# Second attention: even heads' probabilities transposed by VectorE blocks and DMAs, odd heads' by TensorE

## The reference, cut to what matters

```python
    q = (x @ Wq).reshape(b, t, h, dh).transpose(0, 2, 1, 3)
    k = (x @ Wk).reshape(b, t, h, dh).transpose(0, 2, 1, 3)
    wv = _topk_mask(gl_v, SEL) * jax.nn.sigmoid(gl_v)          # gl_v = x @ Ws
    xv = jnp.einsum('btd,edk->btek', x, Wv)
    v = jnp.einsum('bthe,btek->bhtk', wv, xv)
    scores = jnp.einsum('bhid,bhjd->bhij', q * scale, k)
    probs = jax.nn.softmax(scores, axis=-1)
    attn = jnp.einsum('bhij,bhjd->bihd', probs, v)
    mask_o = _topk_mask(gl_o, SEL)                             # gl_o = x @ Wd
    out = jnp.einsum('bthe,bthk,ekd->btd', mask_o, attn, Wo)
```

## Time and profile before

| | |
|---|---|
| Time, median of 3 runs | 1181.05 us (1181.04 to 1181.17) |
| The profiled execution, first to last instruction (its span) | 1179.4 us |
| What lies around the span, by that median | 1.7 us |
| PE busy | 1166.3 us, 99% |
| DVE, ACT, POOL busy | 71%, 55%, 56% |

### The profile page before, as it was taken

The page is one execution under the profiler, slowest core; times in us unless marked ns, Lnnn a source line. Parts: engine busy times, 40 slices in busy tenths (PEclk is TensorE's granted clock), DMA queues, the critical chain, the costliest instruction groups (busy, mean ns, idle before and its releaser), DMA issues.

```text
span 1179.4 us, 19711 instructions
## 1 busy us (share of the span) xinstructions
PE 1166.3 (99%) x6381; PEld 909.4 (77%) x6381; DVE 834.1 (71%) x1524; ACT 650.8 (55%) x1456; POOL 659.0 (56%) x476
## 2 busy tenths in 40 slices
PE   7999999999999999999999999999999999999998
PEld 6888888888888888877767777677677777777765
DVE  7988787878787857465675765666666765765768
ACT  7634343434343434477656666556657666665654
POOL 2635242424242425459298297397397396495595
PEclk9999999999999999999999999999999999999999
DMA  5441423232323224401002002002002011010021
GB/s 198 144 132 46 134 63 115 67 111 73 105 79 99 80 63 155 153 6 37 1 1 107 0 18 89 0 25 81 0 36 71 0 56 51 0 71 0 0 71 37
DMA packets 40893, 75.92 MB, mean 64 GB/s; under 512 B 3744, under 2 KB 4512, under 8 KB 40864
## 3 DMA queue, kind: packets, MB, share of 16 engines
q1 hardware_dynamic: 40864, 75.55, 19.1%
HBM read 58.76 MB, written 16.78 MB: 64 GB/s over the span
## 4 chain that ended last, share of the span: by engine, by line
PE 93%; DVE 4%; ACT 1%; issue 1%; DMA 0%; DVEq 0%
PE ps_f L992 22%; PE ps_r L2081 13%; PE ps_o L2151 9%; PE ps_s L2138 8%; PE ps_s L2130 8%; PE ps_s L992 7%; PE ps_h L992 6%; PE ps_r L2090 6%; PE ps_r L2114 4%; PE ps_r L2096 1%; PE ps_r L2072 1%; PE ps_r L2104 1%; DVE z_tmp L1764 1%; DVE z L1764 1%; PE ps_t L1051 1%
## 5 line engine op out<-in xcount | busy, mean ns | idle before, releaser
L1750 DVE TENSOR_REDUCE nmax<-ps_s 128x1 f32<-128x512 f32 x256 | 158.7, 682 | 112.9 <-PE ps_s L2130 111.9
L1581 ACT ACTIVATE tmp<-ps_s,nmax 128x512 f32<-128x512 f32 x256 | 172.7, 687 | 94.0 <-DVE nmax L1750 94.0
L1524 POOL TENSOR_TENSOR z<-z,z_tmp 128x1280 f32<-128x1280 f32 x35 | 102.9, 2939 | 166.3 <-DVE z_tmp L1764 164.0
L1506 POOL TENSOR_TENSOR spare<-xv,pick 128x512 f32<-128x512 f32 x160 | 169.4, 1059 | 35.6 <-DVE pick L1859 22.7
L1512 POOL TENSOR_TENSOR spare<-spare 128x512 f32<-128x512 f32 x128 | 181.6, 1419 | 10.0
L1590 ACT ACTIVATE pt<-ps_s 128x512 f32<-128x512 f32 x256 | 132.1, 612 | 10.5 <-PE ps_s L2138 10.5
L2138 PE MATMUL ps_s<-ident,tmp 128*128 128x128 f32 x1024 | 122.3, 273 | 0.0
L2138 PEld LDWEIGHTS ps_s<-ident,tmp 128*128 128x128 f32 x1024 | 115.4, 140 | 8.6 <-issue 1.6
L2151 PE MATMUL ps_o<-pt,spare 128*64 128x512 f32 x496 | 113.3, 598 | 0.0
L254 POOL TENSOR_TENSOR e_t<-e_t 128x512 fp32r<-128x512 f32 x28 | 35.4, 1301 | 135.6 <-ACT e_t L510 135.6
L2130 PE MATMUL ps_s<-k,q 64*128 64x512 f32 x768 | 107.0, 409 | 0.1
(11 more groups left out here) (235 smaller groups left out, 2125.4 us busy)
## 6 DMA issues: line engine op xcount, KB each, us to landing
stage<-in_x SPq DMA_DIRECT2D x32, 256.0 KB, 3.3
x_sb<-in_x SPq DMA_DIRECT2D x8, 1024.0 KB, 5.4
x_dram<-x_sb SPq DMA_DIRECT2D x32, 256.0 KB, 3.1
stage<-x_dram SPq DMA_DIRECT2D x8, 1024.0 KB, 5.6
x_sb<-x_dram SPq DMA_DIRECT2D x8, 1024.0 KB, 5.7
out_dram<-x_sb SPq DMA_DIRECT2D x31, 256.0 KB, 2.0
stage<-in_ctx_t SPq DMA_DIRECT2D x28, 256.0 KB, 2.9
stage<-in_ctx SPq DMA_DIRECT2D x28, 256.0 KB, 2.7
```

What stands on the lines that cost most here:

```text
L1506: pool.tensor_tensor(v_tmp[:] if e else acc, xv[:, :, e, :].unsqueeze(2).broadcast_to(shape), pick[:, 0, e, :, 2 * p:2 * p + 2].unsqueeze( ...
L1524: pool.tensor_tensor(zv, zv, z_tmp[:, h % 2], ALU.add).then_inc(z_pool, 1)
L1581: act.activation(probs[:, n % BANKS, :], ps_s[:, n % BANKS, :], ACT.Exp, bias=nmax[:, n:n + 1], accum_out=den[:, h, t:t + 1]).then_inc(p_e ...
L1750: dve.tensor_reduce(nmax[:, n:n + 1], ps_s[:, n % BANKS, :], AX_X, ALU.max, negate=True).then_inc(nmax_ready, 1)
```

## The change

The two tiles of even heads in each round are no longer transposed by PE and copied by ACT. DVE transposes each in place in SBUF, in blocks of 32x32, and then DMAs of SP's queue carry the blocks to the partitions on which they belong in `pt`: 16 DMAs for each round, one for each pair of source and destination quarter of the partitions. Each has 32 partitions with 4 pieces of 64 elements, 256 bytes, so 32 KB. The columns of a head in `pt` are ordered quarter, query tile, element within the block instead of query tile, element; ACT's copy of the odd tiles writes this order, and the copy of the product with v (`out_copy`) puts it back.

The probabilities of even heads have two rounds of buffer (the old `tmp`), those of odd heads one round (a new `probs_odd`). The exponential of an even tile waits for the DMAs of the round two before (`moved`), and `values` waits for the moved blocks of both rounds of its pair. `scores` waits for the copy of the odd tile alone. The last two rounds of the last item go as before, on PE and ACT.

To make room in SBUF, the unused part of `z_t2` is dropped, `halves` becomes the smaller `better` (the count over the experts' comparisons takes 4 additions of 320 elements instead of 3, one of them of 640), and the output mask has its own bf16 buffer `mask` instead of half of `pick`.

```diff
+        def even_probs(n):
+            return probs_even[:, n // BANKS % 2, :, n % BANKS // 2, :]
...
+        def turned(n):
+            h, t = head_tile(n)
+            return pt[:, h % 4].rearrange("p k (q t a) -> p k q t a", q=QUADS, a=BLOCK)[:, :, :, t, :]
...
+        MOVED = QUADS * QUADS * 16
...
+            def move_blocks(b, r, first=False):
+
+                p, tiles = r // 2, slice(r % 2 * 2 * BLOCK, r % 2 * 2 * BLOCK + 2 * BLOCK)
+                sp.wait_ge(blocks_turned, b * ODD_STEPS + (r + 1) * ODD_ROUND)
+                if first and p == 2:
+
+                    sp.wait_ge(o_ps, p - 1)
+                for q in range(QUADS):
+                    for j in range(QUADS):
+                        out = pt[j * BLOCK:(j + 1) * BLOCK, 2 * p % 4].rearrange("p k (q u) -> p k q u", q=QUADS)
+                        sp.dma_start(out[:, :, q, tiles],
+                                     probs_even[q * BLOCK:(q + 1) * BLOCK, r % 2].rearrange(
+                                         "p (k j) s a -> p k j (s a)", j=QUADS)[:, :, j, :]).then_inc(moved[r % 2], 16)
+
             def steady(b, more):
-                if more:
-
-                    sp.wait_ge(yt_ps, b * NT + 2 * NT)
-                    load_x1(b + 2)
+                for r in range(CUT, ROUNDS):
+                    move_blocks(b, r)
+                    if more and r == CUT + 1:
+
+                        sp.wait_ge(yt_ps, b * NT + 2 * NT)
+                        load_x1(b + 2)
+                for r in range(CUT):
+                    move_blocks(b + 1, r)
                 store(b)
...
             def scores_exp(b, n, first):
                 act.wait_ge(nmax_ready, b * STEPS + n + 1)
...
+                if n % 2 == 0:
+                    if n >= 2 * BANKS or not first:
+
+                        act.wait_ge(moved[n // BANKS % 2], (b * PAIRS + n // PAIR) * MOVED)
+                    out, scores = even_probs(n), scores.rearrange("p (j a) -> p j a", a=BLOCK)
...
-                        for tile in range(n * BANKS, n * BANKS + BANKS):
+                        for tile in range(n * BANKS + 1, n * BANKS + BANKS, 2):
                             probs_copy(b, tile, first)
...
+            def turn_blocks(b, n):
+
+                dve.wait_ge(p_exp, b * STEPS + n + 1)
+                dve.transpose(even_probs(n), even_probs(n)).then_inc(blocks_turned, 1)
+
...
                 elif place == TURNS:
+                    if 0 <= n < ROUNDS:
+                        for tile in range(n * BANKS, n * BANKS + BANKS, 2):
+                            turn_blocks(b, tile)
                     if n == LAST_SUMS_AT[0]:
                         mix_sum(b, H - 2)
...
-                pe.wait_ge(pt_ready, b * STEPS + PAIR * p + PAIR)
+                pe.wait_ge(pt_ready, odd_turned(b, PAIR * p + PAIR - 1))
+                for r in range(2):
+                    pe.wait_ge(moved[r], (b * PAIRS + p + 1) * MOVED)
                 pe.wait_ge(v_steps, (b * PAIRS + p + 1) * V_STEPS)
...
                     elif place == TURNS:
-                        for tile in range(n * BANKS, n * BANKS + BANKS):
+                        for tile in range(n * BANKS + 1, n * BANKS + BANKS, 2):
                             turn_probs(b, tile)
```

More of the change, by code:

```diff
@@ L1206, in expert_attention @@
     PLACES = range(5)
+    BLOCK, QUADS = 32, P // 32
     def head_tile(n):
@@ L1348, in expert_attention @@
         pt_ready = sem("pt_ready")
+        blocks_turned = sem("blocks_turned")
+        moved = [sem(f"moved{r}") for r in range(2)]
         o_ps = sem("o_ps")
@@ L1471, in _ @@
             load_x1(1)
+            for r in range(CUT):
+                move_blocks(0, r, True)
             with sp.Fori(0, B - 2) as b:
@@ L1576, in scores_exp @@
                 act.wait_ge(nmax_ready, b * STEPS + n + 1)
-                if n >= BANKS or not first:
-                    act.wait_ge(pt_ps, b * STEPS + n - BANKS + 1)
                 h, t = head_tile(n)
-                act.activation(probs[:, n % BANKS, :], ps_s[:, n % BANKS, :], ACT.Exp, bias=nmax[:, n:n + 1],
+                scores = ps_s[:, n % BANKS, :]
+                if n % 2 == 0:
+                    if n >= 2 * BANKS or not first:
+                        act.wait_ge(moved[n // BANKS % 2], (b * PAIRS + n // PAIR) * MOVED)
+                    out, scores = even_probs(n), scores.rearrange("p (j a) -> p j a", a=BLOCK)
+                else:
+                    if n >= BANKS or not first:
+                        act.wait_ge(pt_ps, odd_turned(b, n - BANKS))
+                    out = probs_odd[:, n % BANKS // 2, :]
+                act.activation(out, scores, ACT.Exp, bias=nmax[:, n:n + 1],
                                accum_out=den[:, h, t:t + 1]).then_inc(p_exp, 1)
@@ L1838, in count_better @@
                 rows = beaten[:].rearrange("p s k j g -> p (s k) j g")
[L1839 to L1841 removed]
+                dve.tensor_tensor(better[:], rows[:, :, 0, :], rows[:, :, 1, :], ALU.add).then_inc(gates, 1)
+                for j in range(2, E - 1):
+                    dve.wait_ge(gates, b * GATES + j - 1)
+                    dve.tensor_tensor(better[:], better[:], rows[:, :, j, :], ALU.add).then_inc(gates, 1)
                 dve.wait_ge(sig_exp, b + 1)
[L1843 to L1844 removed]
+                dve.wait_ge(gates, b * GATES + E - 2)
+                dve.tensor_tensor(logits[:].rearrange("p s k g -> p (s k) g"), better[:], rows[:, :, E - 1, :],
                                   ALU.add).then_inc(gates, 1)
@@ L2173, in values_half @@
                     pe.wait_ge(o_ready, B * PAIRS - 1)
-                out = ps_s[:, 0] if half else ps_o
+                out = (ps_s[:, 0] if half else ps_o)[:, half_cols(0)].rearrange("p (q u) -> p q u", q=QUADS)
                 for k in range(NT):
                     for a in range(2):
-                        end = pe.matmul(out[head_rows(a), half_cols(0)], v_acc[:, p, k, a, :],
-                                        pt[:, p % 2 * 2 + a, k, half_cols(half)], start=k == 0, stop=k == NT - 1)
+                        columns = pt[:, p % 2 * 2 + a, k].rearrange("p (q h u) -> p q h u", q=QUADS, h=2)[:, :, half, :]
+                        end = pe.matmul(out[head_rows(a)], v_acc[:, p, k, a, :], columns, start=k == 0, stop=k == NT - 1)
                 end.then_inc(o_ps, 1)
```

114 lines of the change are left out of this document (73 added, 41 removed).

## The result

The changed kernel takes 1228.47 us (median of 4 runs, 1227.39 to 1228.58) against 1181.05 for the kernel before: ratio 1.0399, 95% interval 1.0384 to 1.0414. The profiled execution's own time is 1227.39, its span 1225.6. I had predicted 1152, faster.

A forecast was written before the change was run, and what follows sets the result against it. PE bounds the kernel before; after the change POOL's chain binds at 81.2 us per item. Savings of 1.5 (start), 25.8 (six items at 4.3) and 1.45 (last item) make 28.8 us: 1152 us, own range 1143 to 1160, wider 1132 to 1190.

The forecast's parts named there:

- SP's price: SP's queue: 0.46 us per issue, 7.4 us per round of 16, hidden in a round of about 10.
- ACT begins to wait at 0.52: Round 1, the tightest: one microsecond left before the exponentials need the buffer; at 0.52 us per issue ACT waits.
- The mechanism itself: Rival, DMAs too slow: SP's queue binds from about 0.63 us per issue; at 0.85, 1380 us; chance 0.13.
- `values` comes two steps after its pair's last round: PE's `values`: two steps after their pair's last round, so the moved blocks have more room than in round 1.
- PE's saving: PE's transposes: half of 1.75 us, 0.875, saved per round; 7.0 us per item, 54.2 in all.
- the rival in which PE stays the bound: Rival, whole kernel: POOL's wait is not what it seems and PE still binds; 1132 us; chance 0.07.
- POOL's chain: Steady loop through POOL to `values` of pair 0: 19.64 + 7.35, 19.3 and 34.94; sum 81.2 us against 85.5.
- 0.16 + 0.75: Second y transpose, position 5: PE already waits 0.16 us for DVE's products; 0.75 us of its saving lost there.
- The first item was to give 1.5 us: Start: ACT's logits copy, now 559.24, done by 559.7 against PE's scores at 561.22; 1.5 us won of 6.
- VectorE's transposes: DVE: two block transposes per round at 0.64 us each, 1.28 us per round, 10.3 per item.
- shut POOL out: Rival: DVE's transposes keep POOL from SBUF, 6.4 us more per item in POOL's run; 1201 us; chance 0.09.
- The transfers: DMAs: blocks land some 2.0 us after issue; packets at 46 ns take 6.6 us per round, within the round.

The follow-up runs named there:

- e1: Kernel before, plus eight series of 16 DMAs behind its end, differing in partitions, pieces and SBUF or DRAM source; 1274.49 us.
- e6: Changed kernel, but each round's blocks go through DRAM: one store and four fetches in place of 16 DMAs; 1160.31 us, ratio 0.9827.
- e2: Changed kernel with 8 DMAs of 64 partitions per round in place of 16 of 32, without the crossing between partitions; 1156.81 us, ratio 0.9795.
- e4: e2 with one of five experts left out of POOL's mixtures; 1152.19 us, ratio 0.9755.
- e7: e6 with round 5 of the last item turned by PE and copied by ACT; 1152.44 us, ratio 0.9759.
- e5: Changed kernel with 4 of a round's 16 DMAs split in two, so 20 per round with the same bytes; 1385.93 us, ratio 1.1734.

## Why the prediction was wrong, by its steps

**The step that failed is SP's price: 0.46 us per issue, taken from the earlier trace rows, where 0.647 was measured.** With it the prediction put the whole of SP's work at nothing, as hidden: 7.4 us per round against a round of about 10, where the issues take 10.4. The row was of loads from DRAM. The prediction called it like these DMAs because it too stood back to back and had two or three dimensions on a side, and didn't ask whether the ends of the transfer matter; e1 shows that they do, and that up to four pieces, the number of partitions and crowding hardly count. By its own reckoning ACT begins to wait at 0.52. The mechanism itself stood among the rivals with the right bound, (85.5 - 5) / 128 = 0.63 per issue. It was met at 0.647, with 6.2 us of stores, loads and the pause between them instead of 5: 128 x 0.647 + 6.2 = 89.0. But I priced the rival midway between two far rows, at 0.85 and 1380 us, and gave it 0.13. A price 3% over its limit was the truth, and the range ended at 1190. At 89.0 us per item the reckoning of that rival gives 1181 + 7 x 3.5 = 1206; the rest of the 47 us is the next step.

**A second step was missed:** I said that `values` comes two steps after its pair's last round. That holds in the loop. In the last item it is the next thing after round 5, and cost 16.2 us here, 8.6 in e6, 4.8 in e2. And in the first item the scores of before (L2130) start at 501.09, 509.57, 518.61, 525.04, 531.74 and 539.00: three rounds in a row shorter than even my 7.4 us of issues, and all shorter than 10.4. 7.0 us were lost there; with 8 DMAs a round (e2) nothing is lost there, the y transposes start at 541.48. "A round of about 10" was the loop's mean, used for stretches in which it is not true.

**PE's saving was sized right for a round, and a part of it did not last.** The transposes between the two halves of the product with `Wo`, before and in e2:

```profile
704.43 1.91 PE L2138 MATMUL ps_s<-ident,tmp 128*128 128x128 f32 x16
706.10 3.90 PE L2114 MATMUL ps_r<-wo,z_t 128*128 128x512 f32 x16
```

```profile
777.52 1.04 PE L2243 MATMUL ps_s<-ident,probs_odd 128*128 128x128 f32 x8
778.32 3.90 PE L2217 MATMUL ps_r<-wo,z_t 128*128 128x512 f32 x16
```

1.91 - 1.04 is 0.87, and so is 1.67 - 0.80 from start to start, the 0.875 of the prediction. (The 1.75 of the earlier trace rows is a piece of the chain, without its overlap with the matmuls ahead of it; 1.04 is one of the timeline, with it. The two can't be compared.) But PE's busy time falls by 5.9 us per item (85.34 - 79.47 in e2), not by 7.0. The transposes of one item take 13.8 us from start to start before and 7.9 in e2: in some rounds PE now comes to the eight of them before ACT's exponentials are done, and they stretch to 1.33 (at 683.43) or stand in their midst for 0.17 (at 738.91). The most of this counts as busy time of PE. In e4, where POOL's wait is gone, it is still there, with the 0.9 at the y transposes, and the rival in which PE stays the bound, at 1132, does not come: 1152.

**What held, once the issues were out of the way.** POOL's chain binds at 81.2 us per item: 81.28 in e2, e6 and e7. Its terms, in e2: from the scores of position 7 (722.14) to those of position 1 (742.26) 20.1 us, I said 19.64; from there to `values` of pair 0 (768.57) 26.3, I said 7.35 + 19.3; from `values` (687.29) to the scores of position 7 (722.14) 34.85, I said 34.94. So the first term was 0.5 too small and the second 0.3 too large; that the sum comes out within 0.1 is in part luck. Within the last term PE waits 0.41 at the second y transpose and not the 0.16 + 0.75 that I had put there; the 0.9 shows only in e4, where nothing else holds PE. The first item was to give 1.5 us: the scores at 561.22 stand at 559.51 in e7, 1.7. Six items of 4.22 are 25.3, and by subtraction 1.4 us more come behind them: 28.4 (1180.82 - 1152.44) against my 28.8. The traced execution of e7 is not the median one, so no trace shows that last 1.4. That e7 lands on the forecast's number shows that POOL's chain was worked out nearly right; it does not make the forecast of the changed kernel right.

**VectorE's transposes:** I took 1.28 us for two; the timeline has 1.29 and 1.30. They don't shut POOL out: POOL's additions have a median of 1286 ns in the changed kernel (L1575) and had 1287 before (L1512), with 124 transposes beside them now. The Trainium skill, "SBUF — State Buffer", "Which ops grab the shared pair", doesn't count the transpose among the one-source operations that take the port pair shared with GpSimd; by that rule the rival falls, and the trace agrees.

**The transfers** land 1.9 us after issue (I said 2.0), and neither their bytes nor their packets bind. The Trainium skill, "DMA: Bandwidth & Descriptors", anatomy of a DMA, has about 2 us of fixed cost for each DMA that GpSimd issues; the prediction used it for SP's queue without saying so. The landing here is near it, and with issues 0.647 us apart it is overlapped by the next ones. What does not overlap is the issue itself on its queue, and for that neither the Trainium skill's 2 us nor its limit of 64 KB gives the number that decided here. The Trainium skill has, in the table of specifications of "DMA: Bandwidth & Descriptors", about 0.6 us on the path from SP, as a latency to the first byte and not as a price per issue; it is near the 0.60 measured, no run shows that the two are one thing, and I didn't weigh it.

## What to carry to other kernels

Many small DMAs from one queue are first of all a count of issues: multiply it by the issue time of a DMA with the same two ends, and compare it with the shortest stretch that it must fit into, not with the loop's mean. A queue has no busy row on the page; look at its timeline for gaps, and if there are none it is the first suspect, however idle the engines and the DMA share look. Then change the number of issues alone, as e2 and e5 do. Giving a part of the issues to another engine's queue was not tried here. When work is moved to a path with more latency, the first and the last iteration need their own check, since the distance between maker and user that the loop gives is missing there. And a rival whose threshold lies near a plausible price deserves the chance that its threshold gives it, and a time near that threshold too.

## What the runs showed of the hardware that was not expected

An issue on SP's queue takes 0.59 to 0.64 us (0.63 to 0.68 from start to start, e1) where both ends are in SBUF, for 32 to 128 partitions and 1 to 4 pieces, and 0.42 to 0.43 us where the source is DRAM (0.46 to 0.50 from start to start); a store of 512 KB to DRAM took 0.33 (e6). The loads of e6, from DRAM with 16 pieces per partition and 128 KB, are 0.65 apart, so many pieces or more bytes do cost something; which of them was not separated.

PE's granted clock fell after waits. In the changed kernel it is 1.00 ahead of the wait of 16.15 us, 0.56 in the mean within it, and 0.72 over the 5.02 us of `values` behind it, which take 3.65 elsewhere. In e4 a wait of 4.6 us was enough, in the windows:

```profile
1113.70:1118.30 4.60, 0.04 (x1) 0.01 (x1) 4.60 (x7) 2.57 (x8) 0.22 (x1) 0.92 0.56 146
1118.30:1125.00 6.70, 6.68 (x17) 1.99 (x18) 1.26 (x1) 0.00 (x0) 2.88 (x1) 0.54 0.01 2
1125.00:1130.00 5.00, 5.00 (x40) 3.61 (x42) 2.20 (x4) 4.13 (x10) 0.00 (x0) 1.00 0.00 0
```

Behind it the clock is 0.54, near the lower of its two levels (1.2 GHz of 2.4), and the same `values` take 6.66 us: the wait costs 4.6 us and then 3.0 more. In e5, where PE idles for up to 4.1 us again and again, the clock is 0.91 over an item, and PE's busy time for the same work is 90.18 us against 80.90. The waits of 0.2 to 1.5 us in the loop of the changed kernel left it at 1.00.

Between these the length of the wait alone did not tell. In the profiled execution of e7 waits of 1.77 and 1.72 us were each followed by a fall: the clock is 0.50 at 561.4 to 563.0 and 0.53 at 1130.7 to 1132.5. In e2 a wait of 2.12 us at the first of these places left it at 1.00. The products behind the first wait in e7 and in e2, and those behind the second in e7, which take 1.95 in the kernel before:

```profile
562.06 3.98 PE L2187 MATMUL ps_r<-es_t,c_t 128*128 128x512 f32 x12
```

```profile
561.63 2.99 PE L2184 MATMUL ps_r<-es_t,c_t 128*128 128x512 f32 x12
```

```profile
1130.71 3.61 PE L2287 MATMUL ps_o<-pt,spare 128*64 128x256 f32 x16 [1.72 <-issue]
```

The other three executions of e7 have a mean clock of 1.000; whether they have the same waits, no trace shows. The Trainium skill, "TensorE: Matmul & The Clock Gate", Part 1, has the clock at its lower level once PE has been idle; the waits of 4.6 and 16.15 us agree with it.
